# Last gated states turned in 32 x 32 squares on VectorE, x1 added by GpSimd instead of a turn in the convolution

## The chip, the cores and the metric
The kernel runs on one core of a Trainium2 chip. The metric is the device time of one execution in microseconds. TensorE (PE) multiplies, VectorE (DVE), ScalarE (ACT) and GpSimd (POOL) work on elements, SyncE (SP) issues the DMA transfers. Each engine takes its instructions in its own order, and they meet through semaphores.

## The reference
Four layers over x of 64 batches x 256 nodes x 128 features, each of the form `x = layernorm(x + layer(x))`, all with the same 256 x 256 adjacency matrix.
```
x = _layernorm(x + attention(x, adj, q, k, v))        # layer 0; gives x1
# layer 1, h starts as x1 and takes 5 steps:
m  = adj @ h                                          # in and out matrix are both adj
z  = sigmoid([m, m] @ w3_w.T + w3_b + h @ u3_w.T + u3_b)
r  = sigmoid([m, m] @ w4_w.T + w4_b + h @ u3_w.T + u3_b)
hv = tanh([m, m] @ w5_w.T + w5_b + (r * h) @ u5_w.T + u5_b)
h  = (1 - z) * h + z * hv
x = _layernorm(x + h)                                 # x1 + h
x = _layernorm(x + sum over powers 0..3 of adj^k @ x @ W_k)      # layer 2, graph convolution
x = _layernorm(x + phi(adj^2-weighted relu(x @ psi), x))         # layer 3, messages
```

## The kernel before
The 64 batches are worked as 32 groups of two. One group is 512 rows (nodes), as four tiles of 128 nodes; in SBUF it is 128 partitions x 512 columns, either by node (nodes in partitions, features in columns) or by feature (turned). Products are made in fp32r, with each operand split into `_hi` and `_lo`, so a result often goes to ACT (`_hi`, a cast) and then to DVE or POOL (`_lo`, the difference).

**Stages.** `attention_layer` makes x1 by node and stores it in `x1_dram`. `gated_layer` takes eight groups as a set (G = 8) through five steps, 40 slots for each of four sets, 160 slots in all. `graph_conv_layers` takes one group in each of 32 slots, with layers 2 and 3 at lags of 1 to 6 slots. The order on each engine is the order of the code of `slot`; `weave` puts the first slots of one stage between the last ones of the stage before, at positions given in lists in `adj_resnorm_d4_kernel`.

**A gated slot.** PE turns `h` (or, in a set's first eight slots, x1) at L731 and multiplies the turned state with adj at L752 and L754 (`m`), then makes the sums for r (L765 to L772), the candidate (L784 to L789) and z (L795 to L797), each at its own lag. ACT casts (`hn_hi` L811 or L813, `m_hi` L822, `rh_hi` L830) and applies sigmoid (L817, L827) and tanh (L834). In a set's first slots ACT also copies the turned x1 to `h` (L810). DVE does, in this order: candidate minus h (L843), `hn_lo` (L847), times z (L853), `m_lo` (L856), r times h (L862), the new h (L866). POOL makes `rh_lo` (L706), `h_hi` (L710) and `h_lo` (L712). SP loads x1 of the next set and stores each final h, by feature, in `h_dram` (L672).

**A convolution slot.** SP loads `ht` (the gated result, by feature) at L1020 and x1 at L1022, behind the output's store of the slot before. PE's order is: the products with the weights for powers 3 and 2 (L1111), features of an older group (L1149, L1152), the turn of `ht` (L1165), weights again, first product with adj (`spread`, L1123 and L1125), messages (L1181, L1183), weights and second spread, the hidden layer (L1193 to L1200), the turn of `x2` (L1211), third spread, outputs (L1220), the turn of `x3` (L1229). Each spread needs `c_hi` (ACT L1312) and `c_lo` (DVE L1426) of the level before. On ACT the four pieces of the output `res` (L1336) stand between `f_hi` (L1326) and the second `c_hi`. DVE adds x1 to the turned `ht` (L1457), makes the sums of the variance (L1469 to L1477) and the normalised `x3` (L1489), and y2 (L1501). POOL takes the power -1/2 of the variances (L1058 for `x3`, L1062 for the others) as soon as `c_var_eps` is there.

## Time and profile before
| | us |
|---|---|
| runs, median of 3 | 1362.06 (1358.49 to 1362.83) |
| profiled execution, its own time | 1361.57 |
| its span, first to last instruction | 1359.8 |
| PE busy | 1328.3 |
| DVE busy | 1084.3 |
| ACT busy | 956.1 |
| POOL busy | 862.6 |

The profile was taken from one execution. The attention stage fills about the first 200 us, the gated stage the time to about 973, the convolution the rest. The granted PE clock is 0.99 of full speed over the span. Busy time counts records that overlap once; a matmul's end is modelled, so the distance between two starts says more on PE than a duration. Behind a row, in square brackets, stands how long its engine was idle before it and what it waited for.

### The profile page before, as it was taken

Reading aid. Unit: us, or ns where it says so; the run is one execution under the profiler, and the core shown is the slowest. Engines: PE = TensorE matmul, PEld = TensorE weight load, DVE = VectorE, ACT = ScalarE, POOL = GpSimd, SP = SyncE. Lnnn points to the kernel's source line nnn. Section 1 sums busy time; section 2 is a strip of 40 time slices with the busy share of each in tenths; the row PEclk is TensorE's granted clock in tenths of the full one; section 3 lists DMA queues with packets and bytes.
Section 4 is the critical chain, followed back from the end, with each engine's and each line's share of the span. In section 5 each row is a group of like instructions: output and inputs, shape, how many; then the busy total and the mean of one; then the engine's idle time right before and its main releaser. Section 6 shows DMA issues by size and latency. Waiting matters only on the chain.

```text
span 1359.8 us, 27644 instructions
## 1 busy us (share of the span) xinstructions
PE 1328.3 (98%) x8638; PEld 1187.0 (87%) x8638; DVE 1084.3 (80%) x2546; ACT 956.1 (70%) x1727; POOL 862.6 (63%) x907
## 2 busy tenths in 40 slices
PE   8999989999999999999999999999899999999997
PEld 7999978888888888888888888887689999999996
DVE  4788878777778777787777887778688888888886
ACT  5788877777777777777777777776546666666664
POOL 5988886666666666666666666666335555555554
PEclk9999999999999999999999999999999999999999
DMA  3333332000020000120000110000212222222211
GB/s 107 93 96 106 97 116 63 1 0 0 23 86 17 0 0 0 39 85 0 0 0 0 55 40 1 0 0 17 70 55 71 71 69 69 69 69 69 69 39 40
DMA packets 60048, 61.25 MB, mean 45 GB/s; under 512 B 4690, under 2 KB 39380, under 8 KB 59988
## 3 DMA queue, kind: packets, MB, share of 16 engines
q1 hardware_dynamic: 59556, 60.31, 14.0%
q8 instruction: 30, 0.49, 0.2%
q10 hardware_dynamic: 432, 0.20, 0.1%
q14 instruction: 30, 0.25, 0.1%
HBM read 35.33 MB, written 25.17 MB: 44 GB/s over the span
## 4 chain that ended last, share of the span: by engine, by line
PE 91%; DVE 3%; ACT 2%; POOL 2%; issue 1%; DVEq 0%; POOLq 0%; ACTq 0%
PE psum L1111 6%; PE psum L752 5%; PE psum L754 5%; PE psum L731 5%; PE psum L379 3%; PE psum L1123 3%; PE psum L1125 3%; PE psum L795 3%; PE psum L784 3%; PE psum L797 3%; PE psum L796 3%; PE psum L767 3%; PE psum L786 3%; PE psum L789 3%; PE psum L772 3%; PE psum L771 3%
## 5 line engine op out<-in xcount | busy, mean ns | idle before, releaser
L706 POOL TENSOR_TENSOR rh_lo<-rh,rh_hi 128x512 fp32r<-128x512 f32 x160 | 206.8, 1293 | 250.9 <-ACT rh_hi L830 250.9
L712 POOL TENSOR_TENSOR h_lo<-h,h_hi 128x512 fp32r<-128x512 f32 x160 | 216.5, 1353 | 12.8
L830 ACT CAST rh_hi<-rh 128x512 fp32r<-128x512 f32 x160 | 99.4, 621 | 140.6 <-DVE rh L862 140.6
L843 DVE TENSOR_TENSOR psum<-psum,h 128x512 f32<-128x512 f32 x160 | 111.9, 700 | 102.9 <-ACT psum L834 102.9
L752 PE MATMUL psum<-adj_t_hi,hn_hi 128*128 128x256 f32 x640 | 164.2, 291 | 1.0 <-DVE m_lo L856 1.0
L754 PE MATMUL psum<-adj_t_hi,hn_lo 128*128 128x256 f32 x640 | 156.6, 280 | 0.0
L827 ACT ACTIVATE psum<-psum,bias_cols 128x512 f32<-128x512 f32 x160 | 106.6, 666 | 60.5 <-PE psum L772 58.7
L862 DVE TENSOR_TENSOR rh<-psum,h 128x512 f32<-128x512 f32 x160 | 110.1, 688 | 45.6 <-ACT psum L827 45.4
L752 PEld LDWEIGHTS psum<-adj_t_hi,hn_hi 128*128 128x128 f32 x640 | 121.0, 189 | 4.9 <-issue 1.8
L754 PEld LDWEIGHTS psum<-adj_t_hi,hn_lo 128*128 128x128 f32 x640 | 120.9, 189 | 3.0
L817 ACT ACTIVATE z<-psum,bias_cols 128x512 f32<-128x512 f32 x160 | 111.6, 698 | 0.0
L853 DVE TENSOR_TENSOR psum<-psum,z 128x512 f32<-128x512 f32 x160 | 110.3, 690 | 0.1
L1312 ACT CAST c_hi<-psum 128x512 fp32r<-128x512 f32 x96 | 56.3, 586 | 76.9 <-PE psum L1125 47.7
L856 DVE TENSOR_TENSOR m_lo<-psum,m_hi 128x512 fp32r<-128x512 f32 x160 | 109.5, 684 | 0.0
L866 DVE TENSOR_TENSOR h<-psum,h 128x512 f32<-128x512 f32 x160 | 108.9, 680 | 0.1
L834 ACT ACTIVATE psum<-psum,bias_cols 128x512 f32<-128x512 f32 x160 | 104.8, 655 | 2.8 <-PE psum L789 2.8
L1123 PE MATMUL psum<-c_hi,adj_t_hi 128*128 128x256 f32 x384 | 99.1, 292 | 5.0 <-DVE c_lo L1426 4.6
L822 ACT CAST m_hi<-psum 128x512 fp32r<-128x512 f32 x160 | 94.8, 592 | 8.1 <-PE psum L754 5.1
L710 POOL CAST h_hi<-h 128x512 fp32r<-128x512 f32 x160 | 98.3, 614 | 0.0
L1125 PE MATMUL psum<-c_lo,adj_t_hi 128*128 128x256 f32 x384 | 94.4, 280 | 0.0
L1058 POOL TENSOR_TENSOR c_rstd<-c_var_eps,c_minus_half 128x4 f32<-128x4 f32 x31 | 31.5, 1017 | 94.1 <-DVE c_var_eps L1477 94.1
L1426 DVE TENSOR_TENSOR c_lo<-psum,c_hi 128x512 fp32r<-128x512 f32 x96 | 65.5, 682 | 29.2 <-ACT c_hi L1312 28.7
(273 smaller groups left out, 4300.3 us busy)
## 6 DMA issues: line engine op xcount, KB each, us to landing
x_in<-in_x_dram SPq DMA_DIRECT2D x32, 256.0 KB, 3.0
x_dram<-x SPq DMA_DIRECT2D x32, 256.0 KB, 2.1
g_x<-x_dram SPq DMA_DIRECT2D x32, 256.0 KB, 3.3
h_dram<-h SPq DMA_DIRECT2D x32, 256.0 KB, 2.0
ht<-h_dram SPq DMA_DIRECT2D x32, 256.0 KB, 2.9
c_x<-x_dram SPq DMA_DIRECT2D x32, 256.0 KB, 3.0
out_dram<-res SPq DMA_DIRECT2D x32, 256.0 KB, 2.4
conv_in<-in_L_gnn_weight_dram SPq DMA_DIRECT2D x1, 448.0 KB, 5.2
```

Source lines behind the costliest of these rows:

```text
L706: pool.tensor_tensor(rh_lo[:, q, :], rh[:, q, :], rh_hi[:, q, :].bitcast(F32), ALU.subtract).then_inc(rh_lo_done, 1)
L712: pool.tensor_tensor(h_lo[:, q, :], h[:, (g - 1) % G, :], h_hi[:, q, :].bitcast(F32), ALU.subtract).then_inc(h_lo_done, 1)
L752: pe.matmul(psum[:, B_M, b * N:(b + 1) * N], hn_hi[:, p, i, :], adj_hi[:, c, :], start=(c == 0), stop=False)
L754: mm = pe.matmul(psum[:, B_M, b * N:(b + 1) * N], hn_lo[:, p, i, :], adj_hi[:, c, :], start=False, stop=(c == KC - 1))
L817: act.activation(z[:, (g - 3) % 2, :], psum[:, B_GATE + (g - 3) % 2, :], ACT.Sigmoid, bias=B_Z).then_inc(z_done, 1)
L843: dve.tensor_tensor(cb, cb, hg, ALU.subtract).then_inc(dif_done, 1)
L853: dve.tensor_tensor(cb, cb, z[:, (g - 4) % 2, :], ALU.mult).then_inc(inc_done, 1)
L856: dve.tensor_tensor(m_lo[:, (g - 1) % 4, :], psum[:, B_M, :], m_hi[:, (g - 1) % 4, :].bitcast(F32), ALU.subtract).then_inc(m_lo_done, 1)
L862: dve.tensor_tensor(rh[:, q, :], psum[:, B_R, :], h[:, (g - 2) % G, :], ALU.mult).then_inc(rh_done, 1)
L866: dve.tensor_tensor(hg, cb, hg, ALU.add).then_inc(h_done, 1)
L1123: pe.matmul(dst, lhs, flat(c_hi[:, level, k * GB:(k + 1) * GB, :]), start=False, stop=False, skip_group_check=True)
L1125: mm = pe.matmul(dst, lhs, flat(c_lo[:, level, k * GB:(k + 1) * GB, :]), start=False, stop=(k == KC - 1), skip_group_check=True)
```

## The change
The gated stage keeps the four tiles of a group in the order (block of nodes, batch) in place of (batch, block). For that the attention stage writes x1 in that order (`by_block`), and the `m` products write their outputs as two runs of 128 columns (`batch`).

After a group's last step DVE turns its `h` in 32 x 32 squares into `squares` (two buffers) one slot after `h` is done, between L843 and `hn_lo` in DVE's order. It waits there for `h_done` and for the store of the group two before. SP stores `squares` in four transfers of 32 partitions each, so that `h_dram` holds the state by node, with runs of 512 bytes. The convolution then needs no turn of `ht` on PE and no sum on DVE: POOL adds x1 (`residual`) into `c_y`, one slot ahead of its use, and SP issues the two loads one slot earlier. `c_y` of groups 0 and 1 is made between POOL's gated slots. ACT waits for the turn, no longer for the store, before it overwrites `h`.

```diff
-                    for _ in weave(both, conv["sync"](sp), [150, 150, 159, 162]):
+                    for _ in weave(both, conv["sync"](sp), [150, 156, 159]):
...
-                    for _ in weave(both, conv["gpsimd"](pool), [155, 159, 162]):
+                    for _ in weave(both, conv["gpsimd"](pool), [152, 153, 155, 159, 162]):
...
         def store(g, k):
-            sp.wait_ge(h_done, k * SET_SLOTS + (SET_SLOTS - G + g + 1))
-            sp.dma_start(h_dram[bass.ds(k * G + g, 1), :, :].rearrange("o p c -> (o p) c"), h[:, g, :])\
-              .then_inc(h_out[g], 16)
+
+            sp.wait_ge(squares_done, k * G + g + 1)
+            nodes = h_dram[bass.ds(k * G + g, 1), :, :].rearrange("o (q i) (a x) -> (o a) i q x", q=QUARTERS, a=QUARTERS)
+            for a in range(QUARTERS):
+                sp.dma_start(nodes[a, :, :, :],
+                             squares[32 * a:32 * a + 32, g % 2, :].rearrange("i (q x) -> i q x", q=QUARTERS))\
+                  .then_inc(h_out[g], 16)
...
                 for b in range(GB):
+                    dst = batch(psum[:, B_M, :], b)
                     for c in range(KC):
...
-                        act.wait_ge(h_out[g], k * 16)
+                        act.wait_ge(squares_done, k * G + (g + 1 - G))
...
+        def turn_squares(g, k):
+
+            dve.wait_ge(h_done, k * SET_SLOTS + (SET_SLOTS - G + g + 1))
+            if isinstance(k, int):
+                wait_count(dve, h_out[(g - 2) % G], 16 * QUARTERS * (k + (0 if g < 2 else 1)))
+            else:
+                dve.wait_ge(h_out[(g - 2) % G], k * (16 * QUARTERS) + (0 if g < 2 else 16 * QUARTERS))
+            dve.transpose(squares[:, g % 2, :].rearrange("p (q t j) -> p t q j", q=QUARTERS, t=TILES),
+                          h[:, g, :].rearrange("p (t q i) -> p t q i", q=QUARTERS, t=TILES)).then_inc(squares_done, 1)
...
+            if final is not None:
+                turn_squares((g - 5) % G, final)
...
+            if live(it, u, -1):
+                load(it + (u + 1) // U, (u + 1) % U)
...
+        def residual(it, u):
+
+            s, q = it * U + u, u % 2
+            pool.wait_ge(y1_loaded[q], it * (32 * U // 2) + 32 * (u // 2 + 1))
+            wait_count(pool, x2_done, s - 1)
+            pool.tensor_tensor(y1[:, q, :, :].rearrange("p i (a j) -> p i a j", a=4),
+                               ht[:, q, :].rearrange("p (a i j) -> p i a j", a=4, i=TILES),
+                               x1[:, q, :, :].rearrange("p i (a j) -> p i a j", a=4), ALU.add).then_inc(y1_done, 1)
...
+            if live(it, u, -1) and not (isinstance(it, int) and s == 0):
+                residual(it + (u + 1) // U, (u + 1) % U)
             pool.wait_ge(var_done, s + 1)
...
-                for b in range(GB):
-                    for c in range(KC):
-                        mm = pe.transpose(psum[:, B_T1, cols(tile(b, c))], ht[:, u % 2, cols(b * KC + c)], ident[:, :])
-                mm.then_inc(y1_mm, 1)
...
-                dve.tensor_tensor(y1[:, u % 2, :, :].rearrange("p (c b) d -> p c b d", c=KC),
-                                  psum[:, B_T1, :].rearrange("p (c b d) -> p c b d", c=KC, b=GB),
-                                  x1[:, u % 2, :, :].rearrange("p (b c) d -> p c b d", b=GB),
-                                  ALU.add).then_inc(y1_done, 1)
                 dve.wait_ge(y1_done, s + 1)
```

On DVE, in two slots at the start of a set (`g_x` is x1, `squares` the turned state), before:
```order
L843 TENSOR_TENSOR psum<-psum,h 128x512
L845 REGISTER_ALU
L847 TENSOR_TENSOR hn_lo<-g_x,hn_hi 128x512
L853 TENSOR_TENSOR psum<-psum,z 128x512
L856 TENSOR_TENSOR m_lo<-psum,m_hi 128x512
L862 TENSOR_TENSOR rh<-psum,h 128x512
L866 TENSOR_TENSOR h<-psum,h 128x512
```
and in the changed kernel, with the line numbers of that kernel:
```order
L872 TENSOR_TENSOR psum<-psum,h 128x512
L864 STREAM_TRANSPOSE squares<-h 128x4x4x32
L878 TENSOR_TENSOR hn_lo<-g_x,hn_hi 128x512
L884 TENSOR_TENSOR psum<-psum,z 128x512
L887 TENSOR_TENSOR m_lo<-psum,m_hi 128x512
L893 TENSOR_TENSOR rh<-psum,h 128x512
L897 TENSOR_TENSOR h<-psum,h 128x512
```
The turn stands ahead of `hn_lo` and of everything behind it in the slot. Eight slots of each set have one.

On POOL, at the passage from the gated stage to the convolution (slots 2 and 3 of the latter and the start of slot 4), before:
```order
L706 TENSOR_TENSOR rh_lo<-rh,rh_hi 128x512 x2
L1062 TENSOR_TENSOR c_rstd<-c_var_eps,c_minus_half 128x4
L1064 TENSOR_TENSOR c_shift<-c_negmean,c_rstd 128x4
L1058 TENSOR_TENSOR c_rstd<-c_var_eps,c_minus_half 128x4
L1062 TENSOR_TENSOR c_rstd<-c_var_eps,c_minus_half 128x4
L1064 TENSOR_TENSOR c_shift<-c_negmean,c_rstd 128x4
L1049 TENSOR_TENSOR x3b<-x,phi_b 128x512
```
and now:
```order
L725 TENSOR_TENSOR rh_lo<-rh,rh_hi 128x512 x2
L1103 TENSOR_TENSOR c_y<-ht,c_x 128x512
L1131 TENSOR_TENSOR c_rstd<-c_var_eps,c_minus_half 128x4
L1133 TENSOR_TENSOR c_shift<-c_negmean,c_rstd 128x4
L1103 TENSOR_TENSOR c_y<-ht,c_x 128x512
L1127 TENSOR_TENSOR c_rstd<-c_var_eps,c_minus_half 128x4
L1131 TENSOR_TENSOR c_rstd<-c_var_eps,c_minus_half 128x4
L1133 TENSOR_TENSOR c_shift<-c_negmean,c_rstd 128x4
L1115 TENSOR_TENSOR x3b<-x,phi_b 128x512
```
The second `c_y` is that of group 4, made in slot 3 ahead of the powers of slot 3.

## Rows read from the trace of the kernel before
**Rows 1.** The page's busy time, share of the span and instructions of each engine.
```profile
PE 1328.3 (98%) x8638; PEld 1187.0 (87%) x8638; DVE 1084.3 (80%) x2546; ACT 956.1 (70%) x1727; POOL 862.6 (63%) x907
```

**Rows 2.** Timeline of PE, a settled convolution slot: start us, length us, what.
```profile
1102.46 0.48 PE L1111 MATMUL psum<-wc_hi,x2t_hi 128*128 128x256 f32 x2
...
1112.36 0.40 PE L1149 MATMUL psum<-psi_row,ones 128*128 128x512 f32 x1
...
1113.84 0.48 PE L1111 MATMUL psum<-wc_hi,x2t_hi 128*128 128x256 f32 x2
...
1117.22 0.33 PE L1123 MATMUL psum<-c_hi,adj_t_hi 128*128 128x256 f32 x1
```

**Rows 3.** Timeline of PE, the last slots of the convolution.
```profile
1317.97 0.40 PE L1149 MATMUL psum<-psi_row,ones 128*128 128x512 f32 x1
...
1319.01 0.48 PE L1111 MATMUL psum<-wc_hi,x2t_hi 128*128 128x256 f32 x2
...
1322.68 0.39 PE L1123 MATMUL psum<-c_hi,adj_t_hi 128*128 128x256 f32 x1
...
1330.30 0.48 PE L1111 MATMUL psum<-wc_hi,x2t_hi 128*128 128x256 f32 x2
```

**Rows 4.** Timeline of ACT in the same slots.
```profile
1319.30 0.60 ACT L1326 ACTIVATE f_hi<-psum 128x512 fp32r<-128x512 f32 x1 [0.54 <-PE psum L1152]
...
1321.33 0.57 ACT L1312 CAST c_hi<-psum 128x512 fp32r<-128x512 f32 x1
```

**Rows 5.** Timeline of DVE in the same slots.
```profile
1321.93 0.69 DVE L1426 TENSOR_TENSOR c_lo<-psum,c_hi 128x512 fp32r<-128x512 f32 x1 [1.31 <-ACT c_hi L1312]
```

**Rows 6.** Timeline of DVE, end of a set and start of the next.
```profile
361.17 0.70 DVE L843 TENSOR_TENSOR psum<-psum,h 128x512 f32<-128x512 f32 x1 [0.65 <-ACT psum L834]
...
365.54 0.70 DVE L843 TENSOR_TENSOR psum<-psum,h 128x512 f32<-128x512 f32 x1 [0.65 <-ACT psum L834]
...
368.83 0.69 DVE L862 TENSOR_TENSOR rh<-psum,h 128x512 f32<-128x512 f32 x1 [0.76 <-ACT psum L827]
...
370.77 0.70 DVE L843 TENSOR_TENSOR psum<-psum,h 128x512 f32<-128x512 f32 x1 [0.65 <-ACT psum L834]
...
385.51 0.70 DVE L843 TENSOR_TENSOR psum<-psum,h 128x512 f32<-128x512 f32 x1 [0.65 <-ACT psum L834]
386.55 1.00 DVE L847 TENSOR_TENSOR hn_lo<-g_x,hn_hi 128x512 fp32r<-128x512 f32 x1 [0.33 <-ACT hn_hi L811]
...
390.59 0.70 DVE L843 TENSOR_TENSOR psum<-psum,h 128x512 f32<-128x512 f32 x1 [0.65 <-ACT psum L834]
```

**Rows 7.** Timeline of POOL, start of that set.
```profile
385.15 1.30 POOL L706 TENSOR_TENSOR rh_lo<-rh,rh_hi 128x512 fp32r<-128x512 f32 x1 [1.52 <-ACT rh_hi L830]
386.39 0.61 POOL L710 CAST h_hi<-h 128x512 fp32r<-128x512 f32 x1
387.08 1.62 POOL L712 TENSOR_TENSOR h_lo<-h,h_hi 128x512 fp32r<-128x512 f32 x1
```

**Rows 8.** Timeline of DVE, passage from the gated stage to the convolution.
```profile
987.31 0.69 DVE L866 TENSOR_TENSOR h<-psum,h 128x512 f32<-128x512 f32 x1
987.92 0.68 DVE L1426 TENSOR_TENSOR c_lo<-psum,c_hi 128x512 fp32r<-128x512 f32 x1
...
994.59 1.11 DVE L1489 TENSOR_SCALAR x<-y,c_negmean,c_rstd 128x128 f32<-128x128 f32 x4
```

**Rows 9.** Timeline of PE in the passage.
```profile
996.45 0.63 PE L1229 MATMUL psum<-ident,x 128*128 128x128 f32 x4 [0.50 <-DVE x2t_lo L1496]
```

**Rows 10.** Timeline of POOL in the passage.
```profile
992.34 1.01 POOL L1058 TENSOR_TENSOR c_rstd<-c_var_eps,c_minus_half 128x4 f32<-128x4 f32 x1 [9.78 <-DVE c_var_eps L1477]
```

**Rows 11.** Timeline of SP's transfers in the passage: start us, issue time us.
```profile
988.03 0.34 SPq L672 DMA_DIRECT2D h_dram<-h  x1
990.49 0.33 SPq L1020 DMA_DIRECT2D ht<-h_dram  x1
```

**Rows 12.** The page's DMA issues: count, KB each, us from issue to landing.
```profile
c_x<-x_dram SPq DMA_DIRECT2D x32, 256.0 KB, 3.0
```

More of the change, by code:

```diff
@@ L749, in slot @@
                 for b in range(GB):
+                    dst = batch(psum[:, B_M, :], b)
                     for c in range(KC):
[L751 to L755 removed]
+                        pe.matmul(dst, hn_hi[:, p, tile(b, c), :], adj_hi[:, c, :], start=(b == 0 and c == 0), stop=False,
+                                  skip_group_check=True)
+                        mm = pe.matmul(dst, hn_lo[:, p, tile(b, c), :], adj_hi[:, c, :], start=False, stop=(c == KC - 1),
+                                       skip_group_check=True)
                 mm.then_inc(m_mm, 1)
@@ L866, in slot @@
                 dve.tensor_tensor(hg, cb, hg, ALU.add).then_inc(h_done, 1)
-        yield from run(dve, slot, 4)
+        for g in range(G):
+            yield g
+            slot(0, g, 0)
+        for k in range(SETS):
+            base = k * SET_SLOTS
+            if k > 0:
+                for g in range(G):
+                    slot(base, g, k, final=(k - 1 if g < 5 else None))
+            with dve.Fori(base + G, base + SET_SLOTS - G, G) as step:
+                for g in range(G):
+                    slot(step, g, None)
+            if k < SETS - 1:
+                for g in range(G):
+                    slot(base + SET_SLOTS - G, g, None, final=(k if g >= 5 else None))
+        for s in range(SLOTS - G, SLOTS + 5):
+            slot(s // G * G, s % G, None, final=(SETS - 1 if s >= SLOTS - G + 5 else None))
+            yield s
     programs = {"sync": sync, "gpsimd": gpsimd, "tensor": tensor, "scalar": scalar, "vector": vector}
     sems = {"h_out": h_out, "hn_lo_done": hn_lo_done, "m_lo_done": m_lo_done, "z_done": z_done,
-            "rh_done": rh_done, "h_done": h_done, "slots": SLOTS, "pairs_end": SLOTS - G}
+            "rh_done": rh_done, "h_done": h_done, "slots": SLOTS, "h_stored": (16 * QUARTERS, 16 * QUARTERS), "pairs_end": SLOTS - G}
     return programs, (earlier, sems)
@@ L966, in graph_conv_layers, with run @@
     res_half_done = sem("res_half_done")
-    def run(eng, slot, second=None):
+    def run(eng, slot, second=None, written_out=0, ahead=0):
         for s in range(PEELED * U):
-            yield s if second is None else 2 * s
+            yield ahead + s if second is None else 2 * s
             slot(s // U, s % U)
@@ L975, in run @@
                 second(s // U, s % U)
-        with eng.Fori(PEELED, GROUPS // U) as it:
+        with eng.Fori(PEELED, GROUPS // U - written_out) as it:
             for u in range(U):
@@ L980, in run @@
                     second(it, u)
+        for s in range(GROUPS - written_out * U, GROUPS):
+            slot(s // U, s % U)
         for u in range(L_W):
@@ L1010, in sync, with load @@
     def sync(sp):
+        def load(it, u):
+            s = it * U + u
+            wait_count(sp, y1_done, s - 1)
+            if isinstance(it, int) and s < U:
+                sp.wait_ge(earlier["h_out"][s], earlier["h_stored"][s % 2])
+            if isinstance(it, int) and s == U:
+                for g, done in enumerate(earlier["h_out"]):
+                    sp.wait_ge(done, earlier["h_stored"][g % 2] * GROUPS // 8)
+            sp.dma_start(ht[:, u % 2, :], h_dram[bass.ds(s, 1), :, :].rearrange("o p c -> (o p) c"))\
+              .then_inc(y1_loaded[u % 2], 16)
+            sp.dma_start(flat(x1[:, u % 2, :, :]), x1_dram[bass.ds(s, 1), :, :].rearrange("o p c -> (o p) c"))\
+              .then_inc(y1_loaded[u % 2], 16)
         def slot(it, u):
             s = it * U + u
-            if live(it, u, 0):
-                wait_count(sp, y1_done, s - 1)
-                if isinstance(it, int) and s < U:
-                    sp.wait_ge(earlier["h_out"][s], 16)
-                if isinstance(it, int) and s == U:
-                    for done in earlier["h_out"]:
-                        sp.wait_ge(done, 16 * GROUPS // 8)
-                sp.dma_start(ht[:, u % 2, :], h_dram[bass.ds(s, 1), :, :].rearrange("o p c -> (o p) c"))\
-                  .then_inc(y1_loaded[u % 2], 16)
-                sp.dma_start(flat(x1[:, u % 2, :, :]), x1_dram[bass.ds(s, 1), :, :].rearrange("o p c -> (o p) c"))\
-                  .then_inc(y1_loaded[u % 2], 16)
+            if isinstance(it, int) and s == 0:
+                load(0, 0)
+            if live(it, u, -1):
+                load(it + (u + 1) // U, (u + 1) % U)
             if live(it, u, L_RES):
@@ L1027, in slot @@
                 sp.dma_start(out_view[:, bass.ds(n * TILES, TILES), :], res[:, u % 2, :, :]).then_inc(res_out[u % 2], 16)
-        yield from run(sp, slot)
+        yield from run(sp, slot, written_out=1)
         for n in range(GROUPS - 4, GROUPS):
@@ L1101, in drain @@
             last_power(LAST, ENTRY + 4)
-        yield from run(pool, slot)
+        for n in range(2):
+            yield n
+            residual(0, n)
+        yield from run(pool, slot, written_out=1, ahead=2)
         drain()
@@ L1206, in slot @@
                 if isinstance(it, int) and n == 0:
-                    pe.wait_ge(y1_done, 2)
+                    pe.wait_ge(earlier["hn_lo_done"], earlier["pairs_end"])
                 if isinstance(it, int) and n == 1:
```

36 lines of the change are left out of this document (15 added, 21 removed).

## The prediction
> **What bounds the kernel now.** The first line of the page has TensorE (PE) busy 98% of the span [rows 1], so a gain has to take time from PE's own queue, and a loss is any time for which PE is made to wait. I read the timelines of the engines next, in four places. In the convolution stage PE repeats one slot every 11.38 us (L1111 at 1102.46 and at 1113.84) with no idle time named [rows 2]. The last slots of that stage are a natural experiment: they already have no turn of `h` and no sum with x1, and there I look at what the slot costs without them [rows 3, 4, 5]. In the gated stage the two places that matter are the slots at the end and the start of a set, since there the new VectorE (DVE) work goes in [rows 6, 7]. Last comes the passage from the gated stage to the convolution, where PE waits already (its records end an idle time of 0.50 us at 996.45) [rows 8 to 12].
>
> **Convolution: what PE loses in work.** The removed four transposes of `ht` (L1165) fill the difference between two distances. With them L1111 follows L1149 after 1113.84 - 1112.36 = 1.48 us [rows 2]; without them after 1319.01 - 1317.97 = 1.04 us [rows 3]. So a slot has 0.44 us less work on PE. If PE were all that mattered, 28 slots (4 to 31) would give 12.3 us. But the slot without the turn goes from L1111 at 1319.01 to L1111 at 1330.30, which is 11.29 us, not 10.94 [rows 3]: only 0.09 us is gained of 0.44. The reason stands in the same slot. From L1111 to the second L1123 it takes 1322.68 - 1319.01 = 3.67 us, where it took 1117.22 - 1113.84 = 3.38 us with the turn [rows 2, 3]. PE waits there for `c_lo`, which waits for ScalarE (ACT): `f_hi` at 1319.30 follows PE's features product (L1152), then come four pieces of `res`, then `c_hi` at 1321.33 [rows 4], then DVE's `c_lo`, 1.31 us idle until 1321.93 [rows 5]. This chain starts at PE's features product, so it moves with PE, and the turn was filling time that PE has to wait anyway. `c_hi` is not sooner because the change leaves `res` in front of it on ACT. The chain exists from slot 6 on (the output lags 6 slots). Sum: slots 6 to 31, 26 x 0.09 = 2.3 us; slots 4 and 5, where no `res` stands in the way, 2 x 0.44 = 0.9 us. Gain 3.2 us.
>
> DVE's sum (0.68 us in each slot) leaves a queue that is idle before `c_lo`: worth nothing by itself. GpSimd (POOL) gets that sum instead. Its like is `rh_lo`, which starts at 385.15 and takes 1.30 us [rows 7], two SBUF sources of 512 elements. The bound above is twice that, 2.6 us, if runs of 32 elements cost POOL more. POOL is busy 63% of the span [rows 1], which leaves over a third of an 11.3 us slot, so either is hidden there by POOL's own idle time; below nothing it can't lie, since POOL only gains work. Where that cover is gone, in the passage, I price it. The loads stand one slot ahead, so none is waited for in a settled slot.
>
> **Gated stage: the new DVE operation.** The trace has no transpose on DVE. The nearest rows are a `tensor_tensor` on the same 512 elements, 0.68 to 0.70 us long, with the next one 0.61 us behind its start (987.31, 987.92) [rows 6, 8], and from SBUF alone the four pieces of `x3`, 1.11 us [rows 8]. I take a step of 0.65 us, near the first, since it also is one pass over 512 elements; the range is 0.6 to 1.1 us.
> The Trainium skill (VectorE: DVE Perf Modes, "The three transpose paths") gives 311 ns for 128 x 128 bf16; scaled by 384 more elements at the page's 0.96 GHz that is 0.71 us, an estimate from the page, which would add 0.06 us to a turn. No row here shows it.
>
> Of each set's eight turns, three fall in ordinary slots. There DVE starts its first operation at 361.17, 365.54, 370.77 [rows 6], a short slot of 4.37 us and a long one of 5.23 in turn. The short one is a closed ring (tanh, DVE's five operations, `rh_hi`, tanh), so the turn lengthens it by 0.65; the long one has 0.76 us idle before `rh` at 368.83 [rows 6], which takes most of it. Over the three: 0.65, then 0.65 + 0.65 - 0.76 = 0.54, then 1.19 us late. PE hardly feels it there, but behind it come eight slots whose ring is 390.59 - 385.51 = 5.08 us [rows 6] against PE's 9.60 / 2 = 4.80 (370.77 - 361.17 is a pair). In them the ring sets the pace, so the lateness reaches PE. I take 1.2 us for each of three boundaries, 3.6 us; below it lies 0, if PE's slack covers it.
>
> The other five turns of a set stand in such ring slots, in front of `hn_lo` (two SBUF sources). There `hn_lo` starts at 386.55 and lasts 1.00 us, against 0.68 to 0.70 of its neighbours; POOL's cast runs beside it until 386.39 + 0.61 = 387.00, and I read the excess as time for which it is held. The turn would be queued at about 385.51 + 0.61 = 386.12 and be over at 386.77, before the cast ends [rows 6, 7]. So it is free, and it stays nearly free up to 0.88 us. Past some 0.95 us POOL's `h_lo` (387.08, 1.62 us) gets in ahead; that is a rival.
>
> The gated `m` products write two runs of 128 columns in place of one of 256. The nearest rows are L1111, whose outputs are cut so already, a pair in 0.48 us, and L1123, which writes 256 in one run, 0.33 us each [rows 2]: per column they are alike, and I cost it at nothing. Before it overwrites `h`, ACT waits for the turn, which is done some slots before, in place of the store: nothing either. SP issues four stores in place of one per group; a set's eight groups have 40 gated slots beside them, so that is hidden, until the last one.
>
> **The passage.** In the trace `h` of the last group ends as DVE goes from 987.31 to `c_lo` [rows 8]; the store goes out at 988.03, the loads for slot 4 at 990.49 [rows 11]. PE's turn of that data stands in slot 4, after the `x3` of 996.45, and found it landed. Now the first to need it is POOL, and in its queue the sum for slot 4 stands in slot 3 ahead of the powers for slot 3, which start at 992.34 now [rows 10]. The reckoning: earlier relief and a turn roughly cancel up to this `h` (the sum leaves two DVE blocks and turns come in); then the last turn, 0.65, to 988.6; four issues 0.4 us apart, the last at 989.9; 2.46 us from issue to load as now (990.49 - 988.03), so 992.3; `c_x` 0.4 us later and 3.0 us to landing [rows 12], 995.7; POOL's sum 1.3, 997.0; the power 1.0, 998.0. `x3` then starts 998.0 - 994.59 = 3.4 us late [rows 8], and PE's turn of `x3` (996.45, waiting already) with it [rows 9]. No slack follows: loss 3.4 us, between 1 (fast stores, more relief before) and 6 (each landing at 4 us).
>
> **Sum.** 1361.57 (the profiled execution's own time; its span is 1359.8) - 3.2 + 3.6 + 3.4 = 1365.4 us. That execution lies 0.5 below the median 1362.06 of the runs; I say 1365. Its own range is 1360 to 1370.
>
> **The rivals.**
> PE's work decides alone: the 0.44 us comes in full, because with DVE and ACT shifted in a slot `c_hi` would be ready sooner. 1361.6 - 12.3 + 3.6 + 3.4 = 1356.3. Against it stands the measured 11.29 us slot. 0.15.
> Turns are covered: the boundaries cost 0 and the passage 1.5. 1361.6 - 3.2 + 1.5 = 1360. 0.12.
> The turn is long (slower): from about 0.95 us `hn_lo` comes behind `h_lo`; at 1.3 us it would start when `h_lo` ends, 387.08 + 1.3 = 388.4, and the ring is 1.5 us longer in 15 slots, 22 us, with 3.1 us instead of 1.2 in each of three boundaries and 1.3 more in the passage: 1365.4 + 22 + 5.7 + 1.3 = 1394. The row of 1.11 us speaks for it, the one-pass rows against. 0.13.
> The turn shares POOL's port: then it queues at 386.12 behind `rh_lo` (until 386.4), holds the cast off, and `hn_lo` comes behind that cast: 0.5 to 0.8 us in 15 slots, 7.5 to 12 us, so 1375. `hn_lo` of 1.00 us beside a cast shows that two-source operations are held so; for one source no row decides. 0.07.
> The Trainium skill (SBUF — State Buffer, "SBUF: two separate sides") says a DVE operation with two SBUF inputs, or with one in a 2-port mode, and a POOL operation exclude each other for their whole length. For the two-source `hn_lo` the trace agrees (1.00 us). It would make this last rival true if the transpose ran in such a mode.
>
> **How the numbers follow.** Forecast 0.53, the four rivals 0.15, 0.12, 0.13, 0.07. The range 1355 to 1376 leaves out the long turn and the ends of the others, under 2 in 10. A measurement can tell about 0.3% (4 us) from no change, so 1358 and 1366 are the marks. Faster: 0.12 of the first rival, 0.04 of the second, 0.02 of the forecast: 0.18. Slower: both slow rivals, 0.20, and 0.17 of the forecast's upper part: 0.37. Same: 0.45.
>
> **What would show it.** Right: L1149 to L1149 in the convolution 11.3 us, with DVE idle before the second `c_lo` and ACT going straight from `res` to it; a set of the gated stage 1.2 us longer; turns of about 0.7 us and `hn_lo` near 0.8 us or less; POOL waiting for a DMA between 990 and 996 and `x3` late. Wrong: slots near 10.95 us, turns over 0.9 us, `hn_lo` over 1.5 us, or POOL's powers at 992 as now.

## The result, and the profile after it

The changed kernel takes 1371.13 us (median of 4 runs, 1370.02 to 1371.61) against 1361.73 us of the kernel before in the same comparison: ratio 1.0072, 95% interval 1.0054 to 1.0090. Two further comparisons, each on another chip, gave 1.0055 (1.0034 to 1.0076) and 1.0059 (1.0046 to 1.0073). Two single runs far above all others, 3366.88 us of the changed kernel in the first of these two and 1883.62 us of the kernel before beside a later experiment, count in no ratio and move the medians given below by 0.1 us at most. So it is slower by 0.6 to 0.7%, some 7.6 us in the last of them (1370.55 against 1362.94 us). The profiled execution took 1370.85 us, its span is 1369.1 us; before, 1361.57 and 1359.8.

The page's busy line, and the two groups of instructions that are new:

```profile
PE 1326.1 (97%) x8510; PEld 1179.1 (86%) x8510; DVE 1082.0 (79%) x2546; ACT 953.2 (70%) x1727; POOL 902.6 (66%) x939
```

```profile
L864 DVE STREAM_TRANSPOSE squares<-h 128x512 f32<-128x512 f32 x32 | 22.4, 702 | 0.0
```

```profile
L1103 POOL TENSOR_TENSOR c_y<-ht,c_x 128x512 f32<-128x512 f32 x32 | 41.3, 1289 | 14.3 <-DMA c_x<-x_dram 14.2
```

Against [rows 1] TensorE has 128 instructions fewer and only 2.2 us less busy time in a span that is 9.3 us longer. The turn takes 702 ns and VectorE never stands idle ahead of it; GpSimd's sum takes 1289 ns, and all its idle time but 0.1 us is a single wait of 14.2 us for a load.

**The gated stage.** Timeline of VectorE (start us, length us, what, idle time before it and its releaser), the end of the first set and a slot of the next, as in [rows 6]:

```profile
363.90 0.70 DVE L872 TENSOR_TENSOR psum<-psum,h 128x512 f32<-128x512 f32 x1 [0.65 <-ACT psum L853]
364.51 0.70 DVE L864 STREAM_TRANSPOSE squares<-h 128x512 f32<-128x512 f32 x1
...
368.83 0.70 DVE L872 TENSOR_TENSOR psum<-psum,h 128x512 f32<-128x512 f32 x1 [0.65 <-ACT psum L853]
...
373.76 0.70 DVE L872 TENSOR_TENSOR psum<-psum,h 128x512 f32<-128x512 f32 x1 [0.65 <-ACT psum L853]
...
378.68 0.70 DVE L872 TENSOR_TENSOR psum<-psum,h 128x512 f32<-128x512 f32 x1 [0.65 <-ACT psum L853]
```

```profile
388.90 0.70 DVE L872 TENSOR_TENSOR psum<-psum,h 128x512 f32<-128x512 f32 x1 [0.65 <-ACT psum L853]
389.51 0.70 DVE L864 STREAM_TRANSPOSE squares<-h 128x512 f32<-128x512 f32 x1
390.13 0.80 DVE L878 TENSOR_TENSOR hn_lo<-g_x,hn_hi 128x512 fp32r<-128x512 f32 x1
...
393.98 0.70 DVE L872 TENSOR_TENSOR psum<-psum,h 128x512 f32<-128x512 f32 x1 [0.65 <-ACT psum L853]
```

```profile
388.54 1.30 POOL L725 TENSOR_TENSOR rh_lo<-rh,rh_hi 128x512 fp32r<-128x512 f32 x1 [1.52 <-ACT rh_hi L849]
```

The next instruction starts 0.62 us behind the start of the turn, even at 389.51, where GpSimd's `rh_lo` runs until 389.84 beside it: no sharing of a port is seen. The three ordinary slots with a turn take 4.93, 4.93 and 4.92 us in place of 4.37, 5.23 and 4.37; the slots with loads of x1 keep 5.08 us. From 363.90 to 388.90 it is 25.00 us, before 385.51 - 361.17 = 24.34: 0.66 us for the boundary. All three boundaries and everything else from the first subtraction of the gated stage to the 151st add 2.0 us.

**The convolution.** TensorE, ScalarE and VectorE in one slot, as in [rows 3 to 5]:

```profile
1303.19 0.48 PE L1183 MATMUL psum<-wc_hi,x2t_hi 128*128 128x256 f32 x2
...
1305.75 0.48 PE L1183 MATMUL psum<-wc_hi,x2t_hi 128*128 128x256 f32 x2
...
1309.41 0.39 PE L1195 MATMUL psum<-c_hi,adj_t_hi 128*128 128x256 f32 x1
...
1314.49 0.48 PE L1183 MATMUL psum<-wc_hi,x2t_hi 128*128 128x256 f32 x2
```

```profile
1306.52 1.64 ACT L1395 ACTIVATE res<-y,c_shift,c_rstd 128x128 f32<-128x128 f32 x4
1308.07 0.56 ACT L1371 CAST c_hi<-psum 128x512 fp32r<-128x512 f32 x1
```

```profile
1308.66 0.69 DVE L1485 TENSOR_TENSOR c_lo<-psum,c_hi 128x512 fp32r<-128x512 f32 x1 [0.54 <-ACT c_hi L1371]
```

The slot is 1314.49 - 1303.19 = 11.30 us long, and the second spread (L1195) starts 1309.41 - 1305.75 = 3.66 us behind the weights: what the last slots of the kernel before had shown (3.67 us). ScalarE goes from `res` to `c_hi` without a gap, and VectorE waits for it. Between the stores of results the settled slots take 11.33 us on the mean, before 11.42.

**The passage.** The last `h` and its turn, SyncE's last stores and the load that stands behind them, GpSimd's sum and power, and `x3`:

```profile
993.82 0.69 DVE L897 TENSOR_TENSOR h<-psum,h 128x512 f32<-128x512 f32 x1
994.55 0.71 DVE L864 STREAM_TRANSPOSE squares<-h 128x512 f32<-128x512 f32 x1
...
1005.11 1.11 DVE L1542 TENSOR_SCALAR x<-y,c_negmean,c_rstd 128x128 f32<-128x128 f32 x4 [2.32 <-POOL c_rstd L1127]
```

```profile
993.23 3.84 SPq L690 DMA_DIRECT2D h_dram<-squares  x8
999.16 0.36 SPq L1069 DMA_DIRECT2D ht<-h_dram  x1
```

```profile
1002.81 1.28 POOL L1103 TENSOR_TENSOR c_y<-ht,c_x 128x512 f32<-128x512 f32 x1 [14.21 <-DMA c_x<-x_dram]
1004.06 1.02 POOL L1127 TENSOR_TENSOR c_rstd<-c_var_eps,c_minus_half 128x4 f32<-128x4 f32 x1
```

From `h` to `x3` it is 11.29 us; in [rows 8] it was 7.28. The chain is the predicted one: last turn, stores, landing, load, sum, power. Two more things stand in the passage that the prediction does not have. The first is before this `h`, on VectorE beside GpSimd:

```profile
959.47 0.82 DVE L1522 TENSOR_TENSOR c_moments<-c_stats 128x36 f32<-128x36 f32 x1
960.22 0.61 DVE L1523 TENSOR_TENSOR c_parts<-c_stats 128x12 f32<-128x12 f32 x1
...
960.95 1.28 DVE L1526 SCALAR_TENSOR_TENSOR c_parts<-c_parts 128x12 f32<-128x12 f32 x1
...
962.34 1.15 DVE L1530 TENSOR_TENSOR c_var_eps<-c_parts 128x12 f32<-128x12 f32 x1
```

```profile
960.88 1.32 POOL L731 TENSOR_TENSOR h_lo<-h,h_hi 128x512 fp32r<-128x512 f32 x1
962.15 1.30 POOL L1103 TENSOR_TENSOR c_y<-ht,c_x 128x512 f32<-128x512 f32 x1
```

Further on, where no GpSimd operation runs beside them, `c_moments` takes 0.19 us and the ones on 12 columns take 0.16 to 0.17 us. Each of the four ends with a GpSimd operation that runs beside it: first `rh_lo` (958.94, 1.29 us), then the cast `h_hi` (960.18, 0.61 us), `h_lo` and the new sum. The kernel before had one such hold in this slot, VectorE and then GpSimd:

```profile
955.87 1.28 DVE L1470 TENSOR_TENSOR c_parts<-c_stats 128x12 f32<-128x12 f32 x1
```

```profile
955.81 1.30 POOL L712 TENSOR_TENSOR h_lo<-h,h_hi 128x512 fp32r<-128x512 f32 x1
```

From `c_moments` to the operation behind `c_var_eps` it is 963.41 - 959.47 = 3.94 us, and in the kernel before 1.88 us (955.75 to 957.63). Only the last of the four holds is the new sum's; the other three meet operations that GpSimd had in the kernel before as well.

The second thing is TensorE's clock. Busy time by stretch (length, then busy us and count of PE, PEld, DVE, ACT, POOL, then granted clock, DMA share, GB/s), first the kernel before, then the changed one:

```profile
990.00:995.00 5.00, 3.91 (x21) 3.38 (x21) 2.51 (x11) 2.03 (x4) 2.18 (x3) 0.72 0.59 201
995.00:1000.00 5.00, 4.50 (x38) 4.28 (x38) 3.47 (x10) 2.78 (x7) 2.08 (x3) 1.00 0.03 12
```

```profile
990.00:995.00 5.00, 2.50 (x21) 2.29 (x20) 4.51 (x10) 0.98 (x3) 0.00 (x0) 0.96 0.13 26
995.00:1000.00 5.00, 3.99 (x17) 3.69 (x18) 2.92 (x13) 0.59 (x1) 0.00 (x0) 0.50 0.39 82
1000.00:1005.00 5.00, 3.15 (x19) 2.71 (x18) 0.77 (x2) 1.08 (x2) 2.19 (x2) 0.84 0.65 210
1005.00:1010.00 5.00, 3.04 (x15) 3.07 (x16) 3.18 (x10) 2.23 (x5) 2.43 (x4) 0.50 0.31 105
```

TensorE is busy for only 2.50 us from 990 to 995, is then granted 0.50 (the level of 1.2 GHz), and gets through 17 records in 3.99 us of work, where the kernel before got through 38 in 4.50 us.

**Where the time went.** Five marks in the timelines cut the span: the first subtraction `cb - hg` of the gated stage, the 151st, the last `h`, the first `x3`, the first store of a result. The mean of two profiles of the kernel before and three of the changed one, in us:

| stretch | before | changed | difference | predicted |
|---|---|---|---|---|
| gated stage, up to the 151st slot | 726.62 | 728.58 | +2.0 | +3.6 |
| passage, up to the last `h` | 59.38 | 61.68 | +2.3 | 0 |
| last `h` to the first `x3` | 7.28 | 11.51 | +4.2 | +3.4 |
| `x3` to the first store of a result | 29.95 | 30.84 | +0.9 | -0.9 |
| from there to the end | 335.03 | 332.80 | -2.2 | -2.3 |
| sum | | | +7.2 | +3.8 |

The sum agrees with the 7.6 us of the last pair of medians. The passage up to the last `h` is the least certain row: it took 60.11 and 58.64 us in the two profiles of the kernel before, and 61.35 to 61.85 in the three of the changed one. The two first profiles differ by 9.3 us because their starts differ too: the first mark lay at 200.68 us before and at 203.41 in the changed kernel. That is not the change, as the repeats show.

### The profile page after: what moved, and what is told of

Its sections match the earlier page's. It is cut to its first block, busy times and chain, and to the rows that moved or that the text cites. A ratio compares the mean times of both kernels' runs of the same rounds, so it can differ in the third digit from the quotient of the medians.

```text
span 1369.1 us, 27592 instructions
## 1 busy us (share of the span) xinstructions
PE 1326.1 (97%) x8510; PEld 1179.1 (86%) x8510; DVE 1082.0 (79%) x2546; ACT 953.2 (70%) x1727; POOL 902.6 (66%) x939
## 4 chain that ended last, share of the span: by engine, by line
PE 81%; ACT 6%; DVE 5%; issue 3%; POOL 1%; DMA 1%; SPq 0%; ACTq 0%; DVEq 0%; POOLq 0%
PE psum L771 5%; PE psum L773 5%; PE psum L750 5%; PE psum L1183 4%; ACT res L1395 3%; PE psum L383 3%; PE psum L814 3%; PE psum L1195 3%; PE psum L803 3%; PE psum L786 3%; PE psum L816 3%; PE psum L815 3%; PE psum L805 3%; PE psum L791 3%; PE psum L808 3%
## 5 line engine op out<-in xcount | busy, mean ns | idle before, releaser
L1195 PE MATMUL psum<-c_hi,adj_t_hi 128*128 128x256 f32 x384 | 101.1, 298 | 9.7 <-DVE c_lo L1485 6.6
L1195 PEld LDWEIGHTS psum<-c_hi,adj_t_hi 128*128 128x128 f32 x384 | 73.4, 191 | 17.2 <-DVE c_lo L1485 17.2
```

Source lines behind the costliest of these rows:

```text
L1195: pe.matmul(dst, lhs, flat(c_hi[:, level, k * GB:(k + 1) * GB, :]), start=False, stop=False, skip_group_check=True)
```

## The experiments

### The same kernels again: what of the difference is chance

No edit: the changed kernel once more, then the kernel before once more, then the changed one a third time.

> The changed kernel once more, nothing edited. In its first profile the gated set began 2.73 us later than in the kernel before: 1.5 us of it in the first slots of the attention, where the granted clock stood at 0.77 to 0.80 from 16 to 24 us, and 1.4 us at 57 us, where TensorE waited 1.38 us before the transposes of x_in. Theory A (chance of one execution): the strided write of x1 costs the attention nothing; this profile has one of the two stalls or none, the first gated convert-and-subtract of the candidate (the one that stood at 203.41 us) begins between 200.7 and 202.5 us, and the median is 1368 to 1370 us. Rival B (the change itself moves the start): it begins at 203.2 to 203.6 us again, with both stalls in the same places, median 1370 to 1371.5 us.

Measured: 1369.21 us (median of 4 runs), ratio 1.0055 (1.0034 to 1.0076). The first mark at 202.17 us, with one of the two stalls, the early granted clock of 0.79.

> The kernel before, unedited, profiled once more. Theory A (what the kernel before showed at the start was one of the lucky executions: the first gated subtraction stood at 200.68 us there, and between 200.6 and 204.2 us in eight other profiles of all kernels): it stands somewhere between 200.5 and 204.3 us again, 33 slots later exactly 160.49 us behind (+-0.02), the four set boundaries and the passage as in the first profile within 0.5 us, and the ratio to the other runs of the kernel before is 1.000 +-0.0015. Rival B (the kernel before starts early as a rule and only the edited ones late): 200.6 to 201.0 us again.

Measured: 1361.94 us, ratio to the other runs of the kernel before 0.9997 (0.9987 to 1.0007). The first mark at 201.02 us; the 34th subtraction 160.48 us behind it, as in all (160.47 to 160.50). The passage up to the last `h` was 1.5 us shorter than in the first profile, more than the 0.5 expected.

> The changed kernel, unedited, a third time, beside the kernel before on the same chip. Theory A (of the 9.3 us between the two first profiles 2.7 are chance of the start, and 5.3 to 6.6 us are the change: 2.0 at the boundaries, 5.2 to 5.8 in the passage, 1.2 to 2.0 us back in the convolution): ratio 1.004 to 1.006. Rival B (the start is part of the change): 1.0065 to 1.0075.

Measured: 1370.55 us, ratio 1.0059 (1.0046 to 1.0073), first mark at 203.88 us.

In twelve profiles the first mark lies between 200.6 and 204.2 us, the latest being one of the kernel before with an edit far behind the attention. A granted clock of 0.79 from 16 to 24 us is in ten of them, and missing in the first profile of the kernel before and in one edit of the changed one. A wait of TensorE for `x_in` near 57 us is in five, of either kernel; in the first profile of the changed kernel it is 1.38 us long. A third stall stands at the end of the attention: from 188 to 192 us the granted clock is 0.57 to 0.80 in eight profiles and 1.00 in the other four (`before_again`, `res_late`, `power_first`, `all_three`), and from the attention's last `p_lo` to the first mark it is 24.56 to 24.78 us in the eight and 23.71 to 23.74 in the four. The kernel before shows it in its first profile and not in its repeat.

Busy time by stretch, 16 to 24 us, in the first profile of the kernel before and in its repeat:

```profile
16.00:24.00 8.00, 5.93 (x49) 5.63 (x48) 4.10 (x9) 5.08 (x7) 6.00 (x8) 1.00 0.03 9
```

```profile
16.00:24.00 8.00, 5.94 (x35) 5.68 (x35) 3.00 (x7) 4.15 (x7) 4.99 (x6) 0.79 0.04 11
```

So theory A holds: 2.7 us of the first two profiles' difference belong to no edit. Over all profiles the first mark lies at 201.97 us on the mean of three with the attention of the kernel before and at 202.19 on the mean of nine with the changed one. The ratio of 1.0059 is at the upper end of what A expected.

### ScalarE's result pieces behind the second c_hi, in both kernels

```
             act.activation(flat(f_hi[:, :, :]), psum[:, B_F, :], ACT.Relu).then_inc(f_hi_done, 1)
+        if live(it, u, L_W):
+            inner_hi(w, 1, a_mm[0])
         if live(it, u, L_RES):
...
             op.then_inc(res_done, 1)
-        if live(it, u, L_W):
-            inner_hi(w, 1, a_mm[0])
```

> The changed kernel with ScalarE's four pieces of the result (res) moved behind the second c_hi of the convolution slot. Theory A (what the prediction says): in a settled slot TensorE waits for spread 1 at the end of the chain features, f_hi, res, c_hi, c_lo, and without res in it the 0.44 us of transposes that the change took from TensorE come out: slots of 10.9 to 11.0 us instead of 11.28, 8 to 10 us in all. Rival B: res then holds msg_hi, and the hidden product of the messages waits instead; slots stay within 0.1 us of 11.28. Rival C: TensorE's own work per slot, not the chain, is 11.28 us (the transposes overlapped something else before); no change either, but with no idle time of TensorE in front of the second spread.

Measured: 1359.79 us (1358.28 to 1361.89, 10 runs), 9.4 us less than the unedited changed kernel on the same chip, ratio to the kernel before 0.9988 (0.9978 to 0.9998). Slots of 10.95 us. TensorE, then ScalarE:

```profile
1295.30 0.48 PE L1183 MATMUL psum<-wc_hi,x2t_hi 128*128 128x256 f32 x2
...
1298.71 0.28 PE L1195 MATMUL psum<-c_hi,adj_t_hi 128*128 128x256 f32 x1
```

```profile
1297.20 0.59 ACT L1371 CAST c_hi<-psum 128x512 fp32r<-128x512 f32 x1 [1.03 <-PE psum L1197]
1297.68 1.65 ACT L1397 ACTIVATE res<-y,c_shift,c_rstd 128x128 f32<-128x128 f32 x4
```

`c_hi` now waits for nothing but the first spread, the second spread starts 3.41 us behind the weights instead of 3.66, and its first product is back at 0.28 us from 0.39. Theory A holds, B and C fall.

> The kernel before with ScalarE's four pieces of the result moved behind the second c_hi of the convolution slot, as in res_late; it keeps TensorE's four transposes of h in each slot. Theory A (the kernel before is bound in the convolution by TensorE's own work, 10.90 us as res_late showed plus the 0.44 us of the transposes = 11.34): slots of 11.33 to 11.36 us instead of 11.38, the run within 2 us of the kernel before (1359.5 to 1361.5 us). Rival B (the chain bound it as well, so the move alone is worth what it was worth in the changed kernel): slots of 11.0 to 11.1 us, 1351 to 1354 us.

Measured: 1359.88 us against 1361.39, ratio 0.9991 (0.9981 to 1.0001). Slots of 11.41 us. The size is a little smaller than A had it (11.42 without the move), and B falls.

The four together, settled slot in us, mean between stores of results:

| | `res` ahead of `c_hi` | `res` behind it |
|---|---|---|
| transposes of `h` on TensorE | 11.42 | 11.41 |
| no transposes | 11.33 | 10.95 |

Neither edit is worth more than 0.1 us alone; together they give 0.47.

### GpSimd's powers ahead of the next group's sum

```
-        if live(it, u, -1) and not (isinstance(it, int) and s == 0):
-            residual(it + (u + 1) // U, (u + 1) % U)
         pool.wait_ge(var_done, s + 1)
...
             pool.tensor_tensor(shift[:, p, late], ...).then_inc(shift_done, 1)
+        if live(it, u, -1) and not (isinstance(it, int) and s == 0):
+            residual(it + (u + 1) // U, (u + 1) % U)
```

> The changed kernel with GpSimd's addition of x1 for the next group moved behind the powers of its slot. Theory A: in the passage from the gated layer to the convolution the powers stood behind an addition that waited 14.2 us for the load behind the last store; with the powers first, x3 of the first group no longer waits for that load. The first x3 then begins about 7.5 us behind the last addition of h instead of 11.3, TensorE is not left at the 0.50 clock, and the kernel is 3.5 to 6 us faster than the changed one (1365 to 1367.5 us). It may also take away the 1.3 us for which VectorE's small operations were held while the first added group ran on GpSimd beside the gated slot. Rival B: the load itself is what is late, since group 4 is needed by the next moments anyway; the wait moves from x3 to the moments of y1 and the gain is under 1.5 us. In settled convolution slots both expect no change (11.28 us, +-0.03).

Measured: 1364.55 us (10 runs, 1361.19 to 1368.86), 4.7 us less than the changed kernel on that chip, ratio to the kernel before 1.0023 (1.0009 to 1.0037).

```profile
996.70 1.02 POOL L1125 TENSOR_TENSOR c_rstd<-c_var_eps,c_minus_half 128x4 f32<-128x4 f32 x1 [10.30 <-DVE c_var_eps L1530]
...
999.68 1.31 POOL L1103 TENSOR_TENSOR c_y<-ht,c_x 128x512 f32<-128x512 f32 x1 [0.71 <-DMA c_x<-x_dram]
```

The power waits for VectorE's variance only; the wait for the load shrank from 14.2 to 0.71 us. `x3` comes 8.88 us behind the last `h` (11.5 without the edit, 7.28 in the kernel before), and the way to that `h` is 0.8 us shorter: the new sum no longer stands beside the small operations, `c_var_eps` is back at 0.17 us, and the slot in which this happens takes 8.64 instead of 9.63 us. The other three holds are still there. Then 1.1 us are given back before the first result, and in this one profile the rest of the span is level. The median says A; the expected 7.5 us was too good, and TensorE's granted clock, at 0.64, 0.68 and 0.66 in the three stretches of 5 us from 990 on, does not stay up as A had it. In the trace the way from the 151st subtraction to the end is only 2.0 us shorter than the mean of the three unedited profiles. Where the other 2.7 us of the medians come from is not shown; this profile's first mark, at 200.9 us, is among the early ones.

### The load of group 4 behind the sixth store instead of the eighth

```
-    for _ in weave(both, conv["sync"](sp), [150, 156, 159]):
+    for _ in weave(both, conv["sync"](sp), [150, 156, 159, 161]):
...
-            if isinstance(it, int) and s < U:
+            if isinstance(it, int) and s < 2 * U:
                 sp.wait_ge(earlier["h_out"][s], earlier["h_stored"][s % 2])
-            if isinstance(it, int) and s == U:
+            if isinstance(it, int) and s == 2 * U:
```

> The changed kernel with one thing moved on SyncE: the load of group 4 is issued behind the sixth of the last set's stores instead of behind the eighth and all landings (it waits for the landing of group 4's own store alone). GpSimd's order stays. Theory A (the last turn, its four stores and their landings hold the load, and the load holds the powers): the load is issued near 982 us instead of 999, the addition of group 4 runs right behind the powers of its slot, x3 is 3.5 to 4.5 us earlier and the run is 4 to 6 us faster than the changed kernel. Rival B (VectorE's own turns and added work make the passage late, the load is not what ends last): under 1 us. Rival C: the stores that land beside the load are delayed by it and the load by them, so that the gain is 1 to 3 us.

Measured: 1366.14 us (7 runs), 3.1 us less than the changed kernel on that chip, ratio to the kernel before 1.0027 (1.0011 to 1.0043).

```profile
982.28 1.58 SPq L1069 DMA_DIRECT2D ht<-h_dram  x1
```

```profile
990.97 1.29 POOL L1103 TENSOR_TENSOR c_y<-ht,c_x 128x512 f32<-128x512 f32 x1 [1.92 <-ACT x L1424]
```

The load goes out at 982.28 instead of 999.16, the sum waits for no load, and `x3` comes 8.01 us behind the last `h`, 3.5 us sooner. The mechanism is A's. In the trace the way from the 151st slot to the end is 4.5 us shorter than the mean of the three unedited profiles; the medians show 3.1 us, below A's 4 to 6 and in C's range. No transfer that is slowed, as C needs it, stands out. The size stays open by about 1.5 us.

### The turn at the end of VectorE's slot, and two turns in place of one

```
             dve.tensor_tensor(cb, cb, hg, ALU.subtract).then_inc(dif_done, 1)
-        if final is not None:
-            turn_squares((g - 5) % G, final)
...
             dve.tensor_tensor(hg, cb, hg, ALU.add).then_inc(h_done, 1)
+        if final is not None:
+            turn_squares((g - 5) % G, final)
```

> The changed kernel with VectorE's turn moved from behind the subtraction at the slot's start to behind the addition of h at its end. In the gated slots VectorE stands idle 0.65 us there, waiting for ScalarE's candidate. Theory A (the 0.63 us step of the turn costs what of it finds no idle time of VectorE): the 3 ordinary slots of each set's end go back to 4.37 and 5.23 us, each of the three boundaries costs 0.0 to 0.1 us instead of 0.66 to 0.74, 1.8 to 2.1 us in all, and the passage gains 0 to 1 us. Rival B (at the boundaries it is the order of VectorE's work behind TensorE, and the turn at the end delays the next candidate's subtraction instead): the boundaries still cost 0.5 us or more each.

Measured: 1367.04 us (5 runs), ratio to the kernel before 1.0038 (1.0024 to 1.0051), where the unedited one had 1.0055 to 1.0072.

```profile
366.85 0.68 DVE L895 TENSOR_TENSOR h<-psum,h 128x512 f32<-128x512 f32 x1
367.44 0.70 DVE L864 STREAM_TRANSPOSE squares<-h 128x512 f32<-128x512 f32 x1
368.18 0.70 DVE L872 TENSOR_TENSOR psum<-psum,h 128x512 f32<-128x512 f32 x1
```

The turn lies just where VectorE stood idle for 0.65 us, and the next subtraction starts 4.37 us behind the last one (363.81). The first boundary takes 24.34 us, exactly as in the kernel before, and up to the 151st subtraction it is 726.56 us against 726.62. Theory A holds for the boundaries; the passage gained nothing, the lower end of what A gave it.

```
+        dve.transpose(spare[:, g % 2, :]...,
+                      h[:, g, :]...)
         dve.transpose(squares[:, g % 2, :]...,
                       h[:, g, :]...).then_inc(squares_done, 1)
```

> The changed kernel with each turn made twice, the first into a spare tile that nobody reads. The turn's step of 0.63 us comes once more in the same place. Theory A (what the prediction says of the slots with x1 loads: a ring of 5.08 us that is not VectorE's own, and its room of about one turn used up): the ordinary slots with a turn go from 4.93 to 5.55 us, 3 x 0.62 = 1.9 us more per boundary, and the five x1 slots go above 5.08 as well, to 5.3 to 5.7 us. Rival B (VectorE has room for a second turn in the x1 slots): these stay at 5.08 us and a boundary costs only 1.9 us more. In both the passage loses 1 to 5 us more.

Measured: 1397.02 us (one run). The three ordinary slots went from 4.93 to 5.52 us, the x1 slots from 5.08 to 6.45. VectorE, then GpSimd, in one of these:

```profile
390.88 0.70 DVE L875 TENSOR_TENSOR psum<-psum,h 128x512 f32<-128x512 f32 x1 [0.65 <-ACT psum L854]
...
392.70 1.58 DVE L881 TENSOR_TENSOR hn_lo<-g_x,hn_hi 128x512 fp32r<-128x512 f32 x1
...
397.33 0.70 DVE L875 TENSOR_TENSOR psum<-psum,h 128x512 f32<-128x512 f32 x1 [0.65 <-ACT psum L854]
```

```profile
392.44 1.29 POOL L732 TENSOR_TENSOR h_lo<-h,h_hi 128x512 fp32r<-128x512 f32 x1
```

Theory A's 5.55 us for the ordinary slots was right, its 5.3 to 5.7 us for the x1 slots too low; B falls. A second step of 0.6 us costs 1.37 us here, because `hn_lo`, at 0.80 us with one turn, now starts 0.26 us behind GpSimd's `h_lo` and takes 1.58 us. This is the mechanism that the prediction gave to a long turn ("Past some 0.95 us POOL's `h_lo` [...] gets in ahead"), at 22 us for 15 slots; here 15 x 1.37 = 20.6 us.

### All four edits together

Besides `res`, the powers and the early load it has the turn at the slot's end.

> The changed kernel with all four edits: result pieces behind the second c_hi, GpSimd's powers ahead of the addition, the load of group 4 behind the sixth store, and the turn at the slot's end. Theory A (the causes are separate places and their gains add up): from the changed kernel's 1369 to 1371 us: 9.4 us for the slots, 4.5 to 6 us for the passage (the load and the powers take away the same wait in part: 4.6 and 3.0 us alone), 2 us for the boundaries: 1352 to 1355 us, 0.5 to 0.7 % below the kernel before. Rival B (in the passage the faster parts wait for each other, TensorE's clock or the last h): 1356 to 1359 us.

Measured: 1349.82 us (median of 6 runs, 1347.56 to 1351.77), ratio to the kernel before 0.9918 (0.9904 to 0.9932), 11.6 us less than the kernel before and about 20 less than the changed one. The five stretches of the table are 726.54, 58.00, 8.43, 32.26 and 320.58 us. Theory A holds in that the gains add up, and the median is 2.2 us below its range. The stretch behind the first result alone is 332.80 - 320.58 = 12.2 us shorter than in the changed kernel, where A had reckoned 9.4 for the slots. From the 151st subtraction to the first result it is 98.69 us, against 96.61 before, so of the passage something is still left:

```profile
993.56 2.07 DVE L1542 TENSOR_SCALAR x<-y,c_negmean,c_rstd 128x128 f32<-128x128 f32 x4
```

```profile
993.97 1.32 POOL L1103 TENSOR_TENSOR c_y<-ht,c_x 128x512 f32<-128x512 f32 x1
```

`x3`, 1.11 us in [rows 8], takes 2.07 with the new sum beside it; it was 2.08 with the powers moved alone, and 1.11 with the load moved alone, where the sum had run 11 us earlier. So moving GpSimd's sum behind the powers moved the hold from VectorE's small operations to `x3`.

## Why the prediction held, and where its sum was off

The forecast was 1365 us, in a range from 1355 to 1376; measured are 1369.2 to 1371.1 us. The range holds it, and the point is 4 to 6 us too low. Of the three results foreseen, "slower" came, to which it gave 0.37, behind the 0.45 for "same". By its own steps:

- **The convolution's settled slots**: right. "Only 0.09 us is gained of 0.44" came out at 0.09, and the chain that it named for the other 0.35 was shown by the two kernels with `res` moved: without `res` in front of `c_hi` the slot is 10.95 us, and the kernel before gains only 0.01 us by the same edit. The rival in which TensorE's work decides alone (0.15) fell with it.
- **Slots 4 and 5, 0.9 us**: wrong in sign. No gain of 0.88 us can be seen; from `x3` to the first result the changed kernel takes 0.9 us more. In that stretch the granted clock is 0.50 from 1005 to 1010 us and 0.83 in the 5 us behind them, where the kernel before has 1.00 in both. How much is the clock and how much the later load was not separated.
- **The turn's price, 0.65 us step**: right, 0.62 to 0.63. The estimate from the Trainium skill (VectorE: DVE Perf Modes, "The three transpose paths"), 0.71 us for the length, is met by the trace's 0.70 us. The long turn (0.13) and the turn that shares GpSimd's port (0.07) fell; two turns showed that the long one's mechanism and price were real.
- **The boundaries, 1.2 us each**: over-priced by almost twice, 0.66 measured. The step that failed is "over the three: 0.65, then 0.54, then 1.19 us late". The slots do not go short, long, short with a turn in each; they settle at 4.93 us each, and the x1 slot behind them, 5.15 in place of 5.31 us, gives 0.16 back. The closed ring with the turn is 9.86 us for two slots against 9.60 of TensorE, so a pair loses 0.26, not 0.54. "Turns are covered" (0.12) was wrong for this place in the slot and right for another: at the slot's end the boundaries cost nothing.
- **The five turns in x1 slots, free**: right, 5.07 to 5.08 us, and `hn_lo` at 0.80 us in place of 1.00.
- **The passage up to the last h, "relief and a turn roughly cancel"**: this is the largest error, 2.3 us. The sentence let GpSimd's sum be hidden by GpSimd's own idle time. GpSimd had that time, but its sum held one of the small VectorE operations that stand ahead of that slot's gated work. The powers put first took back 1.0 us in that slot. Three older GpSimd operations held three more of them. Slot by slot, the one from the 155th to the 156th subtraction takes 9.63 us in place of 8.30, the next two 4.90 and 4.58 to 5.10 in place of 4.32 and 3.86, and the way from the last subtraction to the last `h`, which has a turn in it, 1.92 in place of 1.45; the slot behind the 151st is 0.35 us shorter. So there is a relief and there are turns, as the step says, but they do not cancel. Why VectorE's small operations meet GpSimd's old ones more often in the changed kernel was not tested by an edit of its own.
- **The last h to x3, 3.4 us**: right in every link, with 4.2 us measured on the mean of three profiles and 4.0 in the first. From the last `h` to the load it is 999.16 - 993.82 = 5.3 us against 992.3 - 987.3 = 5.0 reckoned, and the landing, the sum and the power take the rest as priced, within 0.6 us in all. Both edits that cut this chain, one at SyncE and one at GpSimd, brought `x3` forward, by 3.5 and 2.6 us.

The sum was 3.8 instead of 7.2 us: 1.6 too much for the boundaries, and 2.3, 0.8 and 1.8 too little in the 104 us from the 151st slot to the first result, where five engines change from one stage to the next and durations read in a settled slot do not hold. That the error of the sum is only 3.4 us is in part luck, since the boundaries' error has the other sign.

## What to carry to other kernels

Taking work off the busiest engine pays only as far as the second chain in the same slot lets it: look for a slot of the same profile that lacks the work already, measure it, and, where it is hardly shorter, move what stands ahead in that chain. Here 0.44 us of work was worth 0.09 us, and 0.47 after one edit on an engine that was 70% busy. Work that is added to an engine with idle time still has a place in its queue and a port: put it behind what others wait for (the powers), in the idle gap of its engine (the turn at the slot's end), and look at each short operation of the other engine that it will run beside, or that it shifts so that it runs beside something else.

## What the runs showed of the hardware

- VectorE's transpose of 32 x 32 squares on 128 x 512 float32, from SBUF to SBUF, takes 0.70 us, the next instruction 0.62 us behind its start, and it runs beside a GpSimd operation with two SBUF sources without being longer.
- VectorE operations on 12 columns with two SBUF sources take 0.16 to 0.17 us alone, 1.15 to 1.28 us when a GpSimd operation on two SBUF sources of 128 x 512 runs beside them and 0.61 us beside GpSimd's cast; they end with it. The same was seen at `hn_lo` (0.80 and 1.58 us) and the four pieces of `x3` (1.11 and 2.07 us). The Trainium skill (SBUF — State Buffer, "SBUF: two separate sides") states such an exclusion for VectorE operations with two SBUF inputs; the traces agree for those. `x3`, which has one tensor and two columns of scalars as its sources, was stretched too; the section names a 2-port mode as the other case, and no run here shows whether `x3` ran in one.
- GpSimd's sum of two 128 x 512 operands read in runs of 32 columns takes 1.29 us, as its subtraction of the same size in whole rows (`rh_lo`) does.
- The granted clock fell to 0.79 from 16 to 24 us in ten of twelve profiles and not in the other two; the same kernel, the one before, showed 1.00 in one execution and 0.79 in another. From 188 to 192 us it fell (0.57 to 0.80) in eight of the twelve, again in one execution of the kernel before and not in the other. With a wait for `x_in` in five, the start of all that follows lies at 200.6 to 204.2 us.
